# A Mamba, cross-attention and expert layer on one core: state sums as accumulating transposes into a time-major bank

## What is computed

```python
u = silu(causal_conv(x_in))                       # 512 channels, 256 steps
delta = softplus(dt @ dt_proj.T + dt_proj_b)
def step(h, inp):                                 # 16 states for each channel
    d_t, b_t, c_t, u_t = inp
    h = h * exp(d_t[:, :, None] * A) + (d_t * u_t)[:, :, None] * b_t[:, None, :]
    y = einsum('bdn,bn->bd', h, c_t)              # sum over the states
    return (h, y)
...
y = ys.swapaxes(0, 1) + u * D_param               # skip term
y = y * silu(z)                                   # gate
return einsum('bld,ed->ble', y, out_proj_w)
```

## Time and profile before

| | |
|---|---|
| median of three runs | 1122.46 us |
| the profiled execution's own time | 1123.29 us |
| its span, first to last instruction | 1121.5 us |
| TensorE busy (matmuls) | 957.9 us, 85% |
| VectorE busy | 848.6 us, 76% |
| ScalarE busy | 625.9 us, 56% |
| GpSimd busy | 746.0 us, 67% |
| state sums on TensorE (L1104) | 1024 matmul halves, 248.6 us busy |
| scans on VectorE (L1649) | 128, 293.1 us busy |
| products on VectorE (L1656) | 128, 156.0 us busy |

### The profile page before, as it was taken

One profiled execution on the slowest core, in us unless ns is written; L12 is line 12 of the kernel. 1 busy time (PEld: TensorE's weight loads), 2 busy tenths in 40 slices (PEclk: granted clock), 3 DMA queues, 4 the chain that ended last, 5 costly groups with the idle time before them and its releaser, 6 DMA issues. The chain is left out here.

```text
span 1121.5 us, 17555 instructions
## 1 busy us (share of the span) xinstructions
PE 957.9 (85%) x4878; PEld 801.3 (71%) x4878; DVE 848.6 (76%) x1645; ACT 625.9 (56%) x1555; POOL 746.0 (67%) x648
## 2 busy tenths in 40 slices
PE   6598989999999999999987989706989999899475
PEld 4476767888887887887866877605878778787354
DVE  0669999899999999999999994764656555555175
ACT  4766685875874865865864644403545555545100
POOL 1445576748679888888978986564777777777400
PEclk9698999999999999999988999957999999999699
DMA  7472854924124224134133012238998989997596
GB/s 237 169 253 77 252 171 151 300 71 162 45 63 143 76 68 153 62 100 133 40 126 118 37 48 75 101 120 260 326 301 262 297 281 287 285 294 244 187 377 222
DMA packets 118461, 195.48 MB, mean 174 GB/s; under 512 B 17684, under 2 KB 83378, under 8 KB 115922
## 3 DMA queue, kind: packets, MB, share of 16 engines
q1 hardware_dynamic: 79890, 134.54, 37.5%
q0 software_dynamic: 16512, 35.19, 8.6%
q10 hardware_dynamic: 21952, 24.51, 6.8%
HBM read 155.21 MB, written 75.64 MB: 206 GB/s over the span
## 5 line engine op out<-in xcount | busy, mean ns | idle before, releaser
L449 POOL TENSOR_TENSOR inf_all<-bc_all,du 128x1024 f32<-128x1024 f32 x128 | 300.6, 2365 | 102.3 <-DVEq L1647 62.0
L1649 DVE TENSOR_TENSOR_SCAN DA<-DA,inf_all 128x1024 f32<-128x1024 f32 x128 | 293.1, 2289 | 15.8 <-ACT DA L712 12.9
L1104 PE MATMUL Y<-hb_all,ident 128*128 128x256 f32 x1024 | 248.6, 391 | 21.9 <-DVE u L1665 21.6
L2196 POOL DMA_INDIRECT yp_dram<-u,sz x216 | 212.8, 985 | 78.9 <-issue 45.7
L1104 PEld LDWEIGHTS Y<-hb_all,ident 128*128 128x128 f32 x1024 | 197.6, 196 | 55.4 <-DVE u L1665 26.1
L712 ACT ACTIVATE DA<-dl,a_neg 128x255 f32<-128x255 f32 x512 | 211.9, 461 | 0.2
L2263 ACT ACTIVATE u<-DA,sz 128x256 f32<-128x256 f32 x216 | 102.3, 474 | 117.3 <-DMA yp_dram<-u,sz 83.7
L1656 DVE TENSOR_TENSOR hb_all<-DA,bc_all 128x1024 f32<-128x1024 f32 x128 | 156.0, 1219 | 7.9 <-DVE DA L1649 0.5
L2231 PE MATMUL DA<-hb_all,sz 128*128 128x256 f32 x432 | 136.5, 398 | 20.1 <-ACT sz L2256 19.0
L2224 PE MATMUL DA<-sz,hb_all 128*128 128x128 f32 x864 | 133.2, 277 | 3.8 <-issue 3.8
L2224 PEld LDWEIGHTS DA<-sz,hb_all 128*128 128x128 f32 x864 | 114.7, 193 | 4.2 <-issue 4.2
(11 more groups left out here) (453 smaller groups left out, 1599.9 us busy)
## 6 DMA issues: line engine op xcount, KB each, us to landing
hb_all<-in_w_moe SPq DMA_DIRECT2D x216, 256.0 KB
bc_all<-bc_dram SPq DMA_DIRECT2D x32, 1024.0 KB, 5.8
inf_all<-xe_dram SPq DMA_DIRECT2D x216, 140.0 KB
bc_all<-yp_dram SPq DMA_DIRECT2D x16, 1024.0 KB, 6.1
xe_dram<-zeros ACTq DMA_DIRECT2D x2, 7420.0 KB, 25.7
xe_dram<-zeros ACTq DMA_DIRECT2D x1, 7560.0 KB, 26.9
yp_dram<-u,sz POOLq DMA_INDIRECT x216
xt<-in_xT SPq DMA_DIRECT2D x8, 256.0 KB, 6.0
```

What stands on the lines that cost most here:

```text
L449: g.tensor_tensor(inf[(b * NTAU + t) % NI][:, :, :], bc[gr][:, 0, :, :], du[p][:, c, :].unsqueeze(1).to_broadcast([P, SG, T]), ALU.mult).t ...
L1104: ins = mm(Y[:, 0:T], ident[:, :], hb[t % NH][:, n, :], start=gr == 0 and n == 0, stop=gr == NG - 1 and n == SG - 1, skip_group_check=True)
L1649: v.tensor_tensor_scan(da[:, :], da[:, :], inf[(b * NTAU + t) % NI][:, :, :].rearrange("p n t -> p (n t)"), 0.0, ALU.mult, ALU.add).then_i ...
L2196: g.indirect_dma_start(yp_dram, bass.IndirectOffsetOnAxis(ap=pid[:, half * UNROLL + s_:half * UNROLL + s_ + 1], axis=0), ys[s_][:, :], Non ...
```

## The change

The state sum turns the data round. In place of a multiplication with the identity that leaves channels on the partitions, each 128 x 128 block of the products is transposed, and the transposes accumulate in the bank: `YT` holds time on the partitions and channels along the row. A chunk takes these steps now:

- `skip_(c)` (TensorE): u times a diagonal matrix of D opens the bank, in the place of VectorE's multiply-add. Four diagonals `d_tap` are made once, by ScalarE, at the start.
- `sum_(t)`: eight transposes (four states, two halves of time) that add to the bank.
- `yt_out(c)` (ScalarE): copies the bank to SBUF, once the chunk's last sum is done.
- `turned_back(c)` (TensorE): two transposes bring it back, channels on the partitions, into the same bank.
- `y(c)` (VectorE): one instruction, the product with silu(z).

`yt` shares its memory with `hs`, `acc` with `base2`; a wait in `base2_` keeps the latter apart. Several sums change places on TensorE, and the gate of chunk 2 stands ahead of ln3 and ln1 on VectorE.

```diff
+        d_tap = sb("d_tap", [P, NC, P])
...
-        acc = sb("acc", [P, QT, D])
+        yt = hs
+        acc = base2
...
+                if b < L6 and acc_st.at(b - 1, 16, True):
+                    pool.wait_ge(acc_st.sem, acc_st.at(b - 1, 16))
+                pool.sem_inc(tick, 1)
                 g.tensor_tensor(base2[:, :, :], x2a[:, :, :], row(B2), ALU.add).then_inc(aff1_d.sem, 1)
...
+            def yt_out(b, c):
+                act.wait_ge(sum_d.sem, sum_d.at(b, NG * (c + 1)))
+                if yb_f.at(b, c, True):
+                    act.wait_ge(yb_f.sem, yb_f.at(b, c))
+                s.activation(yt[:, :], YT, ACT.Copy).then_inc(yt_c.sem, 1)
...
+            for c in range(NC):
+                ins = s.activation(d_tap[:, c, :], ident[:, :], ACT.Copy, scale=d_par[:, c:c + 1])
             ins.then_inc(k_tap.sem, 1)
...
                     decay(s, p, 1)
+                    yt_out(s - 1, 3)
                     decay(s, p, 2)
...
                     ffn1(s - 2, 0)
                 if exists(s):
+                    yt_out(s, 0)
                     decay(s, p, 6)
...
                     decay(s, p, 9)
+                    yt_out(s, 1)
...
                     decay(s, p, 13)
+                    yt_out(s, 2)
...
+            def skip_(b, p, c):
+                if y_d.at(b, c, True):
+                    pe.wait_ge(y_d.sem, y_d.at(b, c))
+                for q in range(QT):
+                    mm(YT[:, rows_half(q)], u[p][:, c, rows_half(q)], d_tap[:, c, :], start=q == 0, stop=False, skip_group_check=True)
+
             def sum_(b, t):
                 gr, c = t % NG, t // NG
-                if gr == 0:
-                    if y_d.at(b, c, True):
-                        pe.wait_ge(y_d.sem, y_d.at(b, c))
                 pe.wait_ge(outflow_d.sem, outflow_d.at(b, t + 1))
                 for n in range(SG):
-                    ins = mm(Y[:, 0:T], ident[:, :], hb[t % NH][:, n, :],
-                             start=gr == 0 and n == 0, stop=gr == NG - 1 and n == SG - 1, skip_group_check=True)
+                    for q in range(QT):
+                        ins = mm(YT[:, rows_half(q)], hb[t % NH][:, n, rows_half(q)], ident[:, :], is_transpose=True,
+                                 start=False, stop=gr == NG - 1 and n == SG - 1, skip_group_check=True)
                 ins.then_inc(sum_d.sem, 1)
+
+            def turned_back(b, c):
+                pe.wait_ge(yt_c.sem, yt_c.at(b, c + 1))
+                for q in range(QT):
+                    ins = mm(YT[:, rows_half(q)], yt[:, rows_half(q)], ident[:, :], is_transpose=True,
+                             start=q == 0, stop=True, skip_group_check=True)
+                ins.then_inc(yb_f.sem, 1)
...
             def y(b, p, c):
                 dve.wait_ge(gate_d.sem, gate_d.at(b, 1))
-                dve.wait_ge(sum_d.sem, sum_d.at(b, NG * (c + 1)))
-                v.scalar_tensor_tensor(Y[:, 0:T], u[p][:, c, :], d_par[:, c:c + 1], Y[:, 0:T],
-                                       ALU.mult, ALU.add).then_inc(y_du.sem, 1)
-                dve.wait_ge(y_du.sem, y_du.at(b, c + 1))
-                v.tensor_tensor(u[p][:, c, :], Y[:, 0:T], sz[p][:, c, :], ALU.mult).then_inc(y_d.sem, 1)
+                dve.wait_ge(yb_f.sem, yb_f.at(b, c + 1))
+                v.tensor_tensor(u[p][:, c, :], YT, sz[p][:, c, :], ALU.mult).then_inc(y_d.sem, 1)
...
                     delta_u(s + 1, 1 - p)
+                if exists(s):
+                    y(s, p, 2)
                 if exists(s - 2):
                     ln3(s - 2, p)
                 if exists(s - 1):
                     ln1(s - 1)
                 if exists(s):
-                    y(s, p, 2)
                     scan(s, 13)
```

More of the change, by code:

```diff
@@ L152, in decoder_kernel @@
         k_pool = sig("k_pool")
-        k_scaled = sig("k_scaled")
         xt_in = sig("xt_in", 16)
@@ L174, in decoder_kernel @@
         sum_d = sig("sum_d", NTAU)
-        y_du = sig("y_du", NC)
+        yt_c, yb_f = sig("yt_c", NC), sig("yb_f", NC)
         y_d = sig("y_d", NC)
@@ L274, in decoder_kernel @@
         full, used = xin[:, 0, 0:NE], xin[:, 1, 0:1]
+        YT = Y[:, 0:T]
         def pair(bank):
@@ L704, in decay @@
                     if isinstance(b, int) and b == 0:
-                        act.wait_ge(k_scaled.sem, 2)
+                        act.wait_ge(k_conv.sem, 4)
                 if outflow_d.at(b, t - NDA + 1, True):
@@ L1005, in tail @@
             def tail():
+                yt_out(L7, 3)
                 chosen_exp(L5)
@@ L1336, in turn @@
                     shared_out(s - 3)
+                if exists(s - 1):
+                    sum_(s - 1, 15)
                 if exists(s + 1) and s >= 0:
@@ L1339, in turn @@
                 if exists(s - 1):
-                    sum_(s - 1, 15)
+                    turned_back(s - 1, 3)
                 if exists(s + 1) and s >= 0:
@@ L1345, in turn @@
                 if exists(s):
+                    skip_(s, p, 0)
                     sum_(s, 0)
+                    sum_(s, 1)
                 if exists(s - 1):
@@ L1350, in turn @@
                     in_proj(s + 1, 3)
-                if exists(s):
-                    sum_(s, 1)
                 if exists(s - 2):
@@ L1365, in turn @@
                 if exists(s):
-                    sum_(s, 4)
+                    turned_back(s, 0)
                 if s == 0:
@@ L1376, in turn @@
                     ffn1(s - 2, 3)
+                if exists(s):
+                    skip_(s, p, 1)
+                    sum_(s, 4)
                 if exists(s - 1):
@@ L1397, in turn @@
                     ffn2(s - 2, range(6, 10))
+                if exists(s):
+                    turned_back(s, 1)
                 if exists(s - 1):
@@ L1402, in turn @@
                 if exists(s):
+                    skip_(s, p, 2)
                     sum_(s, 8)
@@ L1416, in turn @@
                 if exists(s):
+                    turned_back(s, 2)
+                    skip_(s, p, 3)
                     sum_(s, 12)
@@ L1570, in tail @@
                 ffn1_6(0)
+                turned_back(L7, 3)
                 out7(2)
@@ L1625, in front_vector @@
             dve.wait_ge(a_exp.sem, 1)
-            v.tensor_scalar(a_neg[:, :, :], a_neg[:, :, :], -1.0, None, ALU.mult).then_inc(k_scaled.sem, 2)
+            v.tensor_scalar(a_neg[:, :, :], a_neg[:, :, :], -1.0, None, ALU.mult).then_inc(k_conv.sem, 1)
             def softplus(b, p):
```

## The result

| | before | after |
|---|---|---|
| median | 1123.71 us (4 runs) | 1188.32 us (4 runs) |
| ratio to before | | 1.058, 95% interval 1.055 to 1.062 |
| span of the profiled execution | 1121.5 us | 1185.6 us |
| TensorE / VectorE busy | 957.9 / 848.6 us | 915.6 / 833.9 us |
| state sums on TensorE, busy | 248.6 us | 141.9 us |

The change makes the kernel 5.8% slower, although it takes 42 us of work from TensorE and 15 from VectorE. All of it comes from the turns. From first scan to first scan, turns 0 to 6 last 80.6, 78.2, 90.2, 90.4, 93.7, 93.0 and 86.3 us, where they lasted 75.0, 70.3, 77.1, 79.2, 81.8, 81.1 and 83.0: 65 us more. The stretches ahead of the first scan and behind the last differ by under 1 us.

A forecast was written before the change was run, and what follows sets the result against it. VectorE was taken to bound the kernel, TensorE running behind it. New gate waits less removed work, over all turns, gave +39 us and the clock +6; on 1123.29 that made 1168 us, range 1140 to 1195.

The forecast's parts named there:

- Gates 0 and 1: VectorE's gate multiplies of chunks 0 and 1: predicted to stand 3.1 and 2.2 us a turn for the transposes back.
- Gate 2's path: From v's bias add through both in_projs, sum 11, copy and transposes back: 7.1 us, so VectorE stands 4.6 us.
- clock term: TensorE's in_proj work on the chunk 2 path partly at half clock: 1.5 us in each of four turns, +6.
- VectorE's cover: Work VectorE has left ahead of the gate of chunk 2, a product and delta_u: 2.55 us against the 7.1.
- Turns 0 and 1: First two turns: +1 for turn 0, new waits partly replacing old idle time, and +2.6 for turn 1.
- gate 3: Gate of chunk 3: no new wait, its sum ahead of the convolution, VectorE there some 10 us after the turn's start.
- Inflow 14: GpSimd's inflow behind the roots of ln1, with less VectorE work left to cover it: about 0.5 us a turn.
- turn 6: Turn without an in_proj two batches on, so no stall at the gate of chunk 2: +3.6 us.
- The transposes gain: State sums on TensorE: accumulating transposes taken at 0.109 us each, the pace of plain ones, not 0.216.
- The rivals: Three other outcomes, 21% together: bank turn hidden, 1106 (8%); half of it, near 1125 (6%); clock not holding, near 1245 (7%).
- The bank turn: Rival: TensorE's slack lets all three gates find their chunk turned, only removed work counts, 1106 us; 8%.
- the sum of 1245: Rival: TensorE runs the three gate paths at 1.2 GHz throughout, some 80 us more over turns 2 to 6; 7%.

## Why the prediction held, and where it was off

The predicted 1168 us was 20 short of 1188, inside the range, and the direction and its reason were right: less work on both full engines, a longer path to the gate. Of the 20, 9 lie in turns 2 to 5, 10 in turns 0 and 1, and 1 in turn 7.

- **Gates 0 and 1** were right: 3.1 and 2.2 worked out, 3.17 to 3.19 and 2.45 measured in turns 2 to 6. (The pieces listed for gate 1 add up to 15.5 us, not 15.3, so they give 2.4.) The step that mattered was to follow each path back to a VectorE event and to count TensorE's and ScalarE's queues ahead of it.
- **Gate 2's path** was right and its clock term too small: 1.5 us a turn, where the run with the added matmuls shows 2.5 to 3.3. In turn 4, from the end of v's bias add (448.58) to the gate, it took 10.5 us, not 7.1. The two in_projs, from start to the next start, took 3.45 and 3.14 in place of 1.78 each: 3.0 us more; the transposes back add 0.3. I took 1.5 for this, because turn 4 had kept full clock before. But then TensorE had work while VectorE was late; the change itself made the idle stretches that lower the clock, and that could be read from the path already worked out. Turns 2 to 5 came out at 11.2 to 13.0 us more, not 9.7.
- **VectorE's cover** was 0.29 shorter: delta_u took 1.21 us, not 1.50. Before, it ran beside an addition of GpSimd (407.86 to 409.14) and ended 1.08 us behind it; in turn 4 of the changed kernel nothing runs on GpSimd then.
- **Turns 0 and 1** were the other mis-sized term: +5.5 and +7.9 where I had +1 and +2.6. In turn 0, VectorE waits 3.69, 1.46 and 5.47 us at gates 0 to 2. Of the old idle time (12.3 us in the earlier trace rows) 8.5 stood ahead of scans; 7.6 still stands there, and the new came on top (19.3 idle now). In turn 1, gates 0 to 2 wait 1.88, 2.28 and 4.01, where I had 0.8, nothing and 3.5, and gate 3, which I called covered, waits 0.88 there and 1.70 in turn 2. The clock has a part in this too, and I had charged it to gate 2 of four turns alone: in turn 1 TensorE stood 2.59 us ahead of x_proj and 2.97 ahead of k_, and they took 2.75 and 3.52 us in place of 1.94 and 1.89; in turn 0 they took 3.34 and 3.75. With gate 2's path moved, turn 0 is back at 75.9, within 0.9 of before, and turn 1 at 74.3. k_ of turn 1, before and after:

```profile
158.14 1.89 PE L1184 MATMUL PB<-ct,w_k 128*128 128x256 f32 x8
...
165.79 3.52 PE L1214 MATMUL PB<-ct,w_k 128*128 128x256 f32 x8 [2.97 <-ACT dl L691]
```

- **Inflow 14** cost 0.64 (0.5 predicted), VectorE's busy time fell by 2.28 (2.0 predicted; delta_u's 0.29 is in it), turn 6 +3.3 (+3.6) and turn 7 +0.4 (-1).
- **The transposes gain** as taken. A sum of eight takes 1.04 us busy at full clock, and in 105 of 128 sums the starts were 0.76 or 0.77 us apart from first to last, 0.109 each. They accumulate at the pace of plain ones. TensorE's busy time in turn 4 fell by 5.1 us all the same, not by about 10: the two slow in_projs put 3.0 back.
- **The rivals** fell. The bank turn wasn't hidden at any of the three gates. The clock fell at single places, not throughout: turn 4 ran at 0.96 on the mean, turns 0 and 1 at 0.87 and 0.86. So the sum of 1245, which went by the rule in Part 4 of "TensorE: Matmul & The Clock Gate" in the Trainium skill, is refuted as a time for this kernel. Whether a transpose counts as busy these runs can't tell, since ordinary matmuls stand between the sums.

What the runs add up to, in ratios: the order of gate 2 is worth 3.3% (1.058 to 1.026), gates 0 and 1 with decay 10 another 1.8%, and 1.0% remains between the changed kernel with its gates moved (1.0073) and the skip term alone (0.9972). How that last 1% divides between ScalarE's copy in its queue (the 1.28 at scan 11) and the rest wasn't tried.

## What to carry to other kernels

A cheaper operation on an engine that nobody waits for was worth nothing here, while every engine that is put between a result and its user adds its own queue: work the path out from the event that starts it, and put its steps ahead of work that depends on something late. Give the path's matmuls the lower clock as their bound wherever the path itself makes TensorE stand for microseconds, turn by turn. And expect a removed stall to be paid back in part: look at what it was covering, here a decay behind a copy and small VectorE instructions beside GpSimd.

## What the runs showed of the hardware

- Some VectorE instructions on SBUF were held while GpSimd multiplied. A copy of 16 elements took 1.18 us, and a mask of 320 elements 2.81 as a tensor with a scalar and 3.00 as two tensors, ending 0.03, 0.19 and 0.36 us behind the multiply. With one input in PSUM the mask took 0.49 beside the same multiply, and `FIND_INDEX8` on SBUF took its usual 0.32. The page "SBUF — State Buffer" of the Trainium skill, section "SBUF: two separate sides", says that the two engines hold a shared pair of ports exclusively when VectorE uses a two-port mode, or has two SBUF inputs against a GpSimd instruction that reads SBUF. The traces agree for two SBUF inputs; whether the copy and the mask with a scalar, which have one, ran in a two-port mode no run here shows.
- fp32 transposes accumulate in a bank at 0.109 us each (128 columns), half the 0.216 of a matmul half of 256.
- In turn 4, after 3.44 and 1.93 us of standing, TensorE ran whole in_projs at 0.51 and 0.50 of its clock, and sum 11 between them at 0.99. The same standing didn't always have the same end: in turns 2 and 5 the in_proj behind 1.93 us took 1.99, at full clock, and k_ of turn 4 behind 1.67 us took 1.97. Matmuls that only kept TensorE busy brought both in_projs of turn 4 back to 1.97 and 1.99 us.
